# Two adjacency tiles loaded after GpSimd's scatters, and the front of a graph kernel's edge stage written in another order

## The reference, cut to what matters

```python
agg = zeros((n, n)); scores = full((HEADS, n, n), 0)
att = ((q[sub] * k[obj]).sum(-1) / sqrt(DK)).T     # 10000 edges (sub, obj), 8 heads
scores = scores.at[:, sub, obj].set(att)
mask = (1.0 - adj[:n, :n]).astype(bool)            # adj is the aggregator matrix
scores = where(mask, -inf, scores); scores[:, diag, diag] = 1e-7
attn = softmax(scores, axis=2)
x = x + (attn.sum(axis=0) / HEADS) @ h             # h = relu(layernorm(x))
```

## Time and profile before

| what | value |
|---|---|
| median of 3 runs | 1129.84 us (1123.82 to 1131.23) |
| the profiled execution's own time | 1126.79 us |
| its span in the profile | 1124.9 us |
| TensorE busy | 1040.8 us, 93% |
| VectorE busy | 912.0 us, 81% |
| ScalarE busy | 780.1 us, 69% |
| GpSimd busy | 292.8 us, 26% |
| mean granted TensorE clock | 0.984 |

### The profile page before, as it was taken

One profiled execution on the slowest core, in us unless ns is written; L12 is line 12 of the kernel. 1 busy time (PEld: TensorE's weight loads), 2 busy tenths in 40 slices (PEclk: granted clock), 3 DMA queues, 4 the chain that ended last, 5 costly groups with the idle time before them and its releaser, 6 DMA issues. The chain is left out here.

```text
span 1124.9 us, 25109 instructions
## 1 busy us (share of the span) xinstructions
PE 1040.8 (93%) x10565; PEld 704.0 (63%) x10565; DVE 912.0 (81%) x1262; ACT 780.1 (69%) x815; POOL 292.8 (26%) x303
## 2 busy tenths in 40 slices
PE   1999997899999999999999399999999999999997
PEld 1444443344444444444444289999999999999743
DVE  2355146899999999999881699999999999999466
ACT  1244335777777776776632699999999999999122
POOL 2678650000000000000000144444444444444000
PEclk9999998999999999999999799999999999999999
DMA  9640434322212221100053678888888889889311
GB/s 335 164 29 2 114 74 94 79 68 68 47 41 59 59 68 59 38 20 19 29 185 132 210 173 206 207 209 208 208 206 200 208 210 237 197 202 208 124 69 75
DMA packets 75872, 144.56 MB, mean 129 GB/s; under 512 B 9717, under 2 KB 19314, under 8 KB 73714
## 3 DMA queue, kind: packets, MB, share of 16 engines
q1 hardware_dynamic: 50386, 101.19, 25.3%
q0 software_dynamic: 25376, 41.78, 24.6%
HBM read 92.92 MB, written 25.04 MB: 105 GB/s over the span
## 5 line engine op out<-in xcount | busy, mean ns | idle before, releaser
L1519 ACT ACTIVATE area_h<-area_a,keep 128x2048 fp8e4<-128x2048 f32 x209 | 397.1, 1988 | 8.0 <-PE psum L1671 8.0
L1670 PE MATMUL psum<-s_V,area_h 128*128 128x99 bf16 x3328 | 316.9, 210 | 21.7 <-DVE area_b L1437 17.1
L1670 PEld LDWEIGHTS psum<-s_V,area_h 128*128 128x128 fp8e4 x3328 | 304.1, 98 | 23.9 <-issue 17.8
L1671 PE MATMUL psum<-s_V,area_b 128*128 128x99 bf16 x2048 | 201.6, 210 | 0.0
L1671 PEld LDWEIGHTS psum<-s_V,area_b 128*128 128x128 fp8e4 x2048 | 187.9, 98 | 0.0
L743 PE MATMUL psum<-area_h,f_region 128*128 128x512 f32 x384 | 184.9, 596 | 0.0
L1185 DVE SCALAR_TENSOR_TENSOR f_region<-area_b,s_r,f_region 128x1500 f32<-128x1500 f32 x96 | 170.8, 1780 | 2.2
L1566 DVE TENSOR_TENSOR area_h<-area_h,area_a 128x512 uint32<-128x512 uint32 x256 | 168.6, 691 | 4.4
L1196 DVE CUSTOM_DVE_ANT_0 area_b<-psum,late 128x1500 f32<-128x1500 f32 x96 | 161.1, 1716 | 8.4 <-PE psum L658 8.2
L977 ACT ACTIVATE area_b<-area_b,s_negm 128x1500 f32<-128x1500 f32 x96 | 147.8, 1540 | 23.0 <-DVE s_negm L1196 21.9
L658 PE MATMUL psum<-area_a 64*128 64x512 f32 (+1 forms) x576 | 139.8, 620 | 11.5 <-DVE s_negm L1196 11.3
(11 more groups left out here) (186 smaller groups left out, 1415.4 us busy)
## 6 DMA issues: line engine op xcount, KB each, us to landing
...
rel_planes<-f_h SPq DMA_DIRECT2D x3, 2304.0 KB, 16.0
...
```

Source lines behind the costliest of these rows:

```text
L1519: act.activation(masks[:, j, :], s1b[:, b, :], ACT.Relu, bias=t["s2"][:, n, 0, j:j + 1], scale=BIG, saturate=False).then_inc(signs, 1)
L1670: pe.matmul(out[:, :, 0:DZ], masks[:, j, cols], V[:, b, :, j, 0:DZ], **first)
L1671: last = pe.matmul(out[:, :, DZ:CZ], fars[FAR.index(j)][:, cols], V[:, b, :, j, DZ:CZ], **then)
```

## The change

Tiles 5 and 6 (`NU + 1`, `NU + 2`) are now loaded when the first planes' rows have come in, ahead of tiles 7 and 8, and no adjacency load stands between scatters 30 to 79. The rest of the order follows from that. On TensorE tile 5's quarters are turned after the sixth piece of the third unrelated tile's gather, and the last two pieces, the other quarters and the first projection stand around the score pair 1; tile 6's quarters go into step 0. ScalarE's copies follow the same order. On VectorE the finish of the third unrelated tile and the join of tile r = 1 stand behind the eighth mask, its marking and `measure(2)` in step 0, and the join, clearing and marking of r = 2 between the third and the fourth pair of step 0. The first four masks wait for pieces of the gather (a new semaphore `gathered`) and no longer for its end. In step 0 ScalarE makes `low` for r = 1 at the start and for r = 2 late. Two pairs of semaphores at the end are merged, which changes no wait. The copies of tile 6 in ScalarE's `step` stand as TensorE's turns do, and are cut here.

```diff
 REL = 0x38
 NU = NT - ET
+SECOND = {2: 0, 3: 1, 4: 2, 5: 3}
 PLANE = (0,) + tuple(i % PLANES for i in range(EC - 1))
-LATE_LOADS = {60: ADJ_RING, 74: ADJ_RING + 1}
...
     def turns(n, *ms):
-        return [("w", n - 1, m) for m in ms if 1 <= n <= ET]
-    order = adj(1, NU) + adj(2, 3) + [("h", 0)] + adj(NU + 1) + [("proj", 0), ("one", -1), ("h", 1)] + adj(NU + 2)
+        if n == 0:
+            return [("adj", NU + 2, SECOND[m]) for m in ms if m in SECOND]
+        return [("w", n - 1, m) for m in ms if n <= ET]
+    order = adj(1, NU) + adj(2, 3) + [("h", 0)] + adj(NU + 1) + [("proj", 0), ("one", -1), ("h", 1)]
...
             begin.gpsimd(pool)
-            done = 10 + 4 * ADJ_RING
-            for e, k in LATE_LOADS.items():
-                f.scatter(pool, t, done, e)
-                if k == ADJ_RING:
-                    pool.wait_ge(f.chunk0_ready, 4)
-                    pool.wait_ge(f.own_ready, 1)
-                    f.load_adj(pool, io, k)
-                else:
-                    load_adj(k)
-                done = e
-            f.scatter(pool, t, done, EC)
+            f.scatter(pool, t, 10 + 4 * ADJ_RING, EC)
             pool.wait_ge(f.rel_in[0], 16 * PLANES)
+            pool.wait_ge(f.chunk0_ready, 4)
+            pool.wait_ge(f.own_ready, 1)
+            f.load_adj(pool, io, NU + 1)
+            load_adj(NU + 2)
             for k in range(NU + 3, NT):
                 load_adj(k)
...
+                elif u == NU - 2:
+                    last.then_inc(gathered, 1)
...
                 turn_h(0)
                 score(0, 0)
-                for i in range(8):
+                for i in range(6):
                     gather(2, i)
-                    if i % 2:
-                        turn_adj(NU + 1, i // 2)
+                turn_adj(NU + 1, 0)
+                gather(2, 6)
+                turn_adj(NU + 1, 1)
+                gather(2, 7)
+                score(0, 1)
+                turn_adj(NU + 1, 2)
+                turn_adj(NU + 1, 3)
                 project(0)
-                score(0, 1)
+                score(0, 2)
                 turn_one_and_scores(-1)
                 turn_h(1)
-                turn_adj(NU + 2, 0)
-                score(0, 2)
-                turn_adj(NU + 2, 1)
                 score(0, 3)
-                for q in (2, 3):
-                    turn_adj(NU + 2, q)
...
                 if turned:
                     turn_w(r, 2)
+                if n == 0:
+                    turn_adj(NU + 2, SECOND[2])
                 add_blocks(n, 1)
                 if chunked:
                     turn_adj(ka, 0)
                     score(n + 1, 1)
                 if turned:
                     turn_w(r, 3)
+                if n == 0:
+                    turn_adj(NU + 2, SECOND[3])
                 add_blocks(n, 2)
                 if turned:
                     turn_w(r, 4)
+                if n == 0:
+                    turn_adj(NU + 2, SECOND[4])
                 add_blocks(n, 3)
...
                     act.wait_ge(f.plane_zero[i], 16)
                 relu(0)
                 copy_h(0)
-                for q in range(4):
-                    copy_adj(NU + 1, q)
                 relu(1)
+                count(0)
+                copy_adj(NU + 1, 0)
                 exp(0, 0)
+                copy_adj(NU + 1, 1)
+                exp(0, 1)
+                copy_adj(NU + 1, 2)
+                copy_adj(NU + 1, 3)
+                exp(0, 2)
+                exp(0, 3)
                 projected(0)
-                exp(0, 1)
+                exp(0, 4)
+                exp(0, 5)
                 copy_one_and_scores(-1)
                 copy_h(1)
-                count(0)
-                exp(0, 2)
-                copy_adj(NU + 2, 0)
-                exp(0, 3)
-                copy_adj(NU + 2, 1)
-                exp(0, 4)
-                exp(0, 5)
-                copy_adj(NU + 2, 2)
-                f.make_low(act, 1)
-                copy_adj(NU + 2, 3)
                 exp(0, 6)
                 exp(0, 7)
                 edges(0)
...
-                if n + 2 < ET:
+                if n == 0:
+                    f.make_low(act, 1)
+                elif n + 2 < ET:
                     f.make_low(act, n + 2)
                 relu(n + 2)
                 projected(n + 1)
...
                 if turned:
                     copy_w(r, 7).then_inc(evicted, 1)
+                if n == 0:
+                    f.make_low(act, 2)
                 if scored:
                     exp(n + 1, 6)
...
-                elif hd == 0:
-                    dve.wait_ge(agg, NU - 1)
+                else:
+                    dve.wait_ge(*((gathered, (2, 3, 5, 6)[hd]) if hd < 4 else (agg, NU - 1)))
...
                 for hd in range(HA):
                     mask(0, hd)
-                    if hd == 1:
-                        finish_unrelated(2)
-                        measure(2)
-                    if hd == 3:
-                        f.join_planes(dve, 1)
-                        clear(1)
-                        f.mark_related(dve, 1)
+                finish_unrelated(2)
+                f.join_planes(dve, 1)
+                clear(1)
             def step(n):
-                if n + 2 < ET:
+                if 1 <= n < ET - 2:
                     f.join_planes(dve, n + 2)
                 if n == 1:
                     finish_unrelated(3)
                 if n >= 2:
                     finish(n - 2)
-                if n + 2 < ET:
+                if 1 <= n < ET - 2:
                     clear(n + 2)
                 factors(n)
-                if n + 2 < ET:
+                if n == 0:
+                    f.mark_related(dve, 1)
+                elif n + 2 < ET:
                     f.mark_related(dve, n + 2)
-                if n:
-                    measure(n + 2)
+                measure(n + 2)
                 add_diagonal(n)
                 for p in range(PAIRS):
                     for hd in (2 * p, 2 * p + 1):
                     for hd in (2 * p, 2 * p + 1):
                         if n + 1 < ET:
                             mask(n + 1, hd)
+                    if n == 0 and p == 2:
+                        f.join_planes(dve, 2)
+                        clear(2)
+                        f.mark_related(dve, 2)
             front()
             for n in range(ET):
                 step(n)
```

30 lines of the change are left out of this document (18 added, 12 removed).

## The result

The changed kernel's median is **1131.96 us** over 20 runs (1128.29 to 1135.65), the kernel before has 1129.29 us over 20 runs beside it (1122.08 to 1134.58). The ratio is 1.0036, with an interval of 1.0019 to 1.0053, or +4.1 us (2.1 to 6.0) on 1129.3; the two medians are 2.7 us apart, and I go by the ratio. I had forecast -1.8 us. The measured time lies inside my whole range (1121 to 1134), outside the forecast's own (1127.5 to 1131), and the change counts as "within 1%", but its sign is wrong. The profiled execution took 1128.29 us, with a span of 1126.2.

A forecast was written before the change was run, and what follows sets the result against it. The scatters set when edge attention starts, and VectorE bounds from step 0 on. Earlier factors, step 0's added VectorE work and tile 6's quarters summed as -4.5 + 2.5 + 0.2 = -1.8 us, giving 1128.0 us, range 1121 to 1134.

The forecast's parts named there:

- The scatters and the first join: GpSimd's scatters lose the loads' issue and both holes; VectorE joins r = 0 at 160.3, not 168.8, 8.5 us earlier.
- rival 3: Both scatter holes stay because Sync's transfers make them: join 6.7 us later than forecast, +4.9, 1134.7 us; chance 0.05.
- Tile 5 and the third gather: On TensorE: six gather pieces done at 165.6, a 1.0 us wait for tile 5, score pair 1 at 169.7.
- rival 2: Tile 5 lands late, after 9.1 us, and TensorE idles in the gather: +4.0, 1133.8 us; chance 0.18.
- Pairs 1 and 2: On TensorE: the projection, no longer hidden, makes pair 2 start 2.5 us after its masks allowed it.
- Pair 3: Score pair 3 waits for ScalarE's copy behind the sixth exponential: TensorE idle about 4 us, start 186.9, pair 4.2 us.
- The gap and the factors: VectorE's third unrelated finish and r = 1 join precede step 0's factors, which start at 197.3, not 201.8: 4.5 us earlier.
- Step 0: VectorE's join, clearing and marking of r = 2 cost +2.5 us, TensorE's quarters of tile 6 +0.2; later steps unchanged.
- The sum: Whole kernel: -4.5 + 2.5 + 0.2 = -1.8 us, forecast 1128.0 us from the median 1129.8; chance 0.52.
- Rival 1: The clock stays up at pair 3 and tile 5 lands in 5.1 us: -4.1, 1125.7 us; chance 0.20.

The follow-up runs named there:

- x_later: The changed kernel with Sync loading x tiles 1 and 2 only behind the first two stores of chunks; 1129.88 us, ratio 1.0020 against the kernel before.
- again_after: The changed kernel run and profiled a second time with no edit; 1131.75 us, ratio 1.0025 against the kernel before.
- no_sync_at_end: The changed kernel with Sync's three transfers at 152 us issued behind the planes of r = 0 and 1; 1133.82 us, ratio 1.0044.
- proj_early: copy_first with TensorE's first projection moved ahead of tile 5's first quarter, into the wait for that tile; 1126.69 us, ratio 0.9981.
- copy_first: The changed kernel with ScalarE's copies of w12's scores and the turned h ahead of the fifth exponential; 1128.78 us, ratio 1.0004.
- tile5_sooner: The changed kernel with tile 5's load issued directly behind the last scatter, ahead of the wait for the planes; 1133.18 us, ratio 1.0033.
- joins_in_holes: proj_early with VectorE's third unrelated finish behind mask two, r = 1's join behind the fourth, r = 2's before the factors; 1125.63 us, ratio 0.9966.

## Why the prediction was wrong, step by step

**The scatters and the first join: the step that failed.** I had -8.5 us with the bounds -9.0 and -1.8; it was -4.1. Both holes were to vanish, with 0.5 us for a landing of 3.2 beside Sync's transfers. In fact the first hole only shrank: 4.75 and 4.59 us in the two profiles before, 2.18 and 3.01 after, with small ones behind them (0.74, and 0.44 and 0.66; the usual pause is 0.30). The second went from 3.04 and 3.35 to none and 1.93, and where it was gone, the last landing took 3.45 us. On the join that is some two thirds of the price of rival 3, to which I gave 0.05 (+4.4 of its +6.7). Its mechanism, Sync's transfers, is shown for the second hole: in the two kernels without Sync's three transfers at 152 us there is no hole, and the landing takes 2.7 and 3.0 us. Of the ten profiles with late loads and with those transfers, six have a hole of 1.65 to 2.23 us there, and the other four have none but took 3.45 to 3.90 us for the last landing. What leaves 2 to 3 us of the first hole stays open: x_later moved a part of it a few scatters on and won nothing in sum, and no other transfer was moved there. I had argued that "both holes stand right behind a load". They did, and the loads made a part of each; but that was no proof that they made all of it. For the second hole there was another cause beside them, for which the traffic at 137 to 140 us was no stand-in. I had written that the rule of the Trainium skill (DMA: Bandwidth & Descriptors, section SWDGE vs HWDGE vs iDMA) would make Sync's own traffic slow the scatters. The runs agree with it at the second hole (landings of 3.45 to 3.90 us or a hole beside them, 2.7 and 3.0 us without), and the that I held against it were too far from both places.

**Tile 5 and the third gather: right, with a longer wait.** TensorE had the six pieces of the gather done at 165.1 and 165.7 us (165.6 forecast). But the load is issued behind the join and was late with it. Its landing, 5.2 and 5.3 us, was sooner than my 6.0 and within the rows' bounds, and the first quarter was turned 5.6 us after the join (168.39 - 162.81; 6.3 forecast), so the wait was 3.30 and 6.35 us and not 1.0. From the join to pair 1 it took 8.8 us (9.4 forecast), and 11.5 in again_after, where the longer wait cost the clock. That part of rival 2 came without a late landing, by way of the late join; a tile that came more than 7 us after its load's issue was seen only in no_sync_at_end.

**Pairs 1 and 2: right.** Pair 2 came 8.52 us after pair 1 in both profiles (8.6 forecast), because of the projection, which proj_early took away.

**Pair 3: right in its mechanism.** The idle time was 4.22 us (forecast "about 4"), pair 2 to 3 took 9.06 and 8.94 (8.6 forecast), the pair itself 5.30 and 4.09 (4.2). copy_first shows that the copy caused the wait.

**The gap and the factors: right.** Join to f0 was +4.0 us against the kernel before, in the means, as forecast. This rests partly on luck: I had 37.0 - 33.0, and the means are 38.3 and 34.3, so both ends were 1.3 too low and it cancels. Against my one profile before, which had a favourable clock, it would have been +5.3.

**Step 0: right, but it doesn't end there.** +2.4 was measured (35.75 against 33.35), with +2.7 forecast. Step 1 takes 1.0 us more in the profile after and 0.8 in the second one, where I had said that the later steps are as they were. The other profiles say what this 1 us is. Five kernels besides the changed one kept the join of r = 2 in step 0: copy_first and proj_early, in which the pair ahead of step 1 took 4.48 us, have 34.4 us for step 1; x_later, no_sync_at_end and tile5_sooner, in which it took 2.79, have 33.43. TensorE's timeline of no_sync_at_end shows the same idle time as the row at 234.19, and the pair behind it at full clock:

```profile
236.91 0.44 PE L705 MATMUL psum<-ident,f_region 128*128 128x128 f32 x2 [2.36 <-ACT f_h2T L957]
237.28 2.79 PE L655 MATMUL psum<-area_a 64*128 64x512 f32 x12
```

So the 1 us of step 1 goes with the low clock of that one pair, which came in four of the seven profiles with this idle time (2.06 to 2.36 us); in these profiles the idle time alone costs step 1 nothing. (Step 0 itself took 35.7 to 35.8 us in five of the seven; in x_later and tile5_sooner it took 36.4 and 36.7, with 5.37 us for the first pair of r = 1 ahead of it.) In joins_in_holes the idle time is 1.18 us, the pair takes 2.79, and step 1 has 33.43 as well.

**The sum.** -4.1 + 4.0 + 3.3 = +3.2, in place of -8.5 + 4.0 + 2.7 = -1.8. Rival 1 did not occur: tile 5 came early, but the clock fell at pair 3 in both profiles. Where it did stay up, in the one profile of proj_early, the join to f0 takes 30.8 us, though there neither the projection nor the copy holds a pair any more.
